# A graph and expert network on one Trainium2 core: ScalarE normalises every fourth tile of each LayerNorm

## The reference, cut to what matters

```python
def _layernorm(x, axis=-1, eps=1e-05):
    m = jnp.mean(x, axis=axis, keepdims=True)
    v = jnp.var(x, axis=axis, keepdims=True)
    return (x - m) / jnp.sqrt(v + eps)

x = x + L0_gnn(_layernorm(x));  x = x + L0_ffn(_layernorm(x))
x = x + L1_gnn(_layernorm(x));  x = x + L1_ffn(_layernorm(x))
...                             # the same for L2 and L3
```

## Time and profile before

| | us |
|---|---|
| median of three runs | 5675.14 |
| the profiled execution's own time | 5700.08 |
| its span | 5698.0 |
| PE busy | 4359.2 (77%) |
| DVE busy | 3235.9 (57%) |
| ACT busy | 2114.7 (37%) |
| POOL busy | 1202.7 (21%) |

### The profile page before, as it was taken

The page is one execution under the profiler, slowest core; times in us unless marked ns, Lnnn a source line. Parts: engine busy times, 40 slices in busy tenths (PEclk is TensorE's granted clock), DMA queues, the critical chain, the costliest instruction groups (busy, mean ns, idle before and its releaser), DMA issues. The chain is left out here.

```text
span 5698.0 us, 58897 instructions
## 1 busy us (share of the span) xinstructions
PE 4359.2 (77%) x18640; PEld 2870.1 (50%) x18640; DVE 3235.9 (57%) x6106; ACT 2114.7 (37%) x4158; POOL 1202.7 (21%) x1467
## 2 busy tenths in 40 slices
PE   1447355996784988879998898998787596889477
PEld 1335244775111767767775222223576465666366
DVE  7867244114897559731115898995787245453423
ACT  0003122113783045522223887888555011111222
POOL 1566666650220001000000111110010210000142
PEclk9868777997787989979998898899898798999788
DMA  8204243116443745320001443443453235462276
GB/s 351 103 1 162 93 134 88 39 38 208 158 155 113 241 167 196 117 45 0 0 0 58 157 156 124 165 159 94 164 191 128 88 109 177 148 199 90 107 221 203
DMA packets 460063, 733.30 MB, mean 129 GB/s; under 512 B 114081, under 2 KB 258974, under 8 KB 453004
## 3 DMA queue, kind: packets, MB, share of 16 engines
q1 hardware_dynamic: 410012, 690.18, 36.8%
q0 software_dynamic: 30096, 19.30, 1.2%
q10 hardware_dynamic: 19680, 20.48, 1.1%
HBM read 587.26 MB, written 147.21 MB: 129 GB/s over the span
## 5 line engine op out<-in xcount | busy, mean ns | idle before, releaser
L1459 PE MATMUL l2g_a_agg_acc<-all_x,l2g_a_h 128*65 128x512 f32 (+1 forms) x1400 | 644.3, 585 | 23.8 <-ACT l2g_a_agg_flat L1484 21.1
L429 POOL DMA_INDIRECT table<-first_count,first_cell x416 | 449.0, 1079 | 385.9 <-DVE first_cell L377 148.8
L1556 DVE SCALAR_TENSOR_TENSOR all_x<-all_x,l2g_a_agg_counts 128x512 f32<-128x512 f32 (+1 forms) x700 | 404.6, 625 | 121.6 <-ACT all_x L1507 121.0
L1496 ACT ACTIVATE l2g_a_agg_z<-l2g_a_agg_z 128x512 f32<-128x512 f32 (+1 forms) x700 | 344.3, 538 | 141.1 <-PE l2g_a_agg_z L1439 115.8
L1507 ACT ACTIVATE all_x<-l2g_a_agg_z 128x512 f32<-128x512 f32 (+1 forms) x700 | 353.7, 569 | 0.1
L2039 DVE SCALAR_TENSOR_TENSOR all_x<-l1f_moe_py,l1f_gate,all_x 128x256 f32 x200 | 96.7, 483 | 442.5 <-PE l1f_moe_py L1996 442.5
L892 PE MATMUL l3g_agg_acc<-l3g_agg_halves,l3g_agg_exact 128*128 128x512 f32 x1250 | 304.4, 398 | 51.6 <-DVE l3g_agg_exact L945 46.6
L1459 PEld LDWEIGHTS l2g_a_agg_acc<-all_x,l2g_a_h 128*65 128x65 f32 x1400 | 169.3, 144 | 285.9 <-issue 206.1
L1690 PE MATMUL l1g_gat_agg_acc<-l1g_gat_h,l1g_gat_agg_p 128*128 128x257 f32 x1250 | 284.8, 388 | 21.1 <-DVE l1g_gat_agg_p L1777 14.2
L1690 PE MATMUL l2g_b_agg_acc<-l2g_b_h,l2g_b_agg_p 128*128 128x257 f32 x1250 | 283.3, 387 | 19.6 <-DVE l2g_b_agg_p L1777 12.8
L2023 ACT ACTIVATE l1f_moe_hid<-l1f_moe_ph,l1f_vec 128x640 f32<-128x640 f32 x160 | 141.3, 883 | 420.9 <-PE l1f_moe_ph L2010 420.9
(11 more groups left out here) (790 smaller groups left out, 9264.8 us busy)
## 6 DMA issues: line engine op xcount, KB each, us to landing
l3g_agg_counts<-table SPq DMA_DIRECT2D x250, 320.0 KB, 3.4
l2g_a_agg_counts<-table SPq DMA_DIRECT2D x300, 256.0 KB, 4.4
table<-counting_eye_rows SPq DMA_DIRECT2D x25, 1600.0 KB, 37.3
l0g_agg_counts<-table SPq DMA_DIRECT2D x125, 320.0 KB
l1g_agg_counts<-table SPq DMA_DIRECT2D x125, 320.0 KB, 3.4
l2g_a_mask<-far SPq DMA_DIRECT2D x50, 800.0 KB, 4.4
l1g_gat_agg_counts<-table SPq DMA_DIRECT2D x150, 256.0 KB, 3.9
l2g_b_agg_counts<-table SPq DMA_DIRECT2D x150, 256.0 KB
```

The costliest lines, as they stand in the source:

```text
L429: pool.indirect_dma_start(self.table, bass.IndirectOffsetOnAxis(ap=self.cell[:, b, p:p + 1], axis=0), self.count(b, p), None, bounds_check ...
L1459: pe.matmul(to, rhs(t, r * per + h), p[:, u % n_p, 0:n], start=(t == 0), stop=(t == nt - 1), skip_group_check=True).then_inc(summed, 1)
L1496: act.activation(z[:, u % nz, 0:n], z[:, u % nz, 0:n], ACT.Relu, scale=1.0 - SLOPE).then_inc(bent, 1)
L1556: dve.scalar_tensor_tensor(out=w, in0=w, scalar=1.0, in1=counts[:, b % n_counts, 0:n], op0=ALU.min, op1=ALU.mult).then_inc(weighted, 1)
```

## The change

In each LayerNorm, ACT normalises the tiles with t % 4 == 3 (six of the 25), as Identity(scale * x + bias) with scale = rstd and bias = -mean * rstd, both columns of one number a row. DVE computes that bias for all tiles in one instruction of 128x25 (`shift`) and normalises the other 19 tiles. ACT does tiles 3 and 7 before its first copy, and tile 11, 15, 19 and 23 behind its copies 0, 2, 4 and 6; in `l3g_ln` it does all six in a row. `turn_tiles` waits for DVE's count and, at each fourth tile, for ACT's. A LayerNorm stage has 11 semaphores where it had 9.

```diff
+        shift = s.sb("shift", [P, T])
...
+                dve.scalar_tensor_tensor(out=shift[:], in0=mv[:, :, 0], scalar=-1.0, in1=rstd[:], op0=ALU.mult, op1=ALU.mult
+                                         ).then_inc(shifted, 1)
                 for t in range(T):
-                    dve.tensor_scalar(xn[:, t, :], x[:, t, :], mv[:, t, 0:1], rstd[:, t:t + 1],
-                                      ALU.subtract, ALU.mult).then_inc(done, 1)
+                    if t % 4 != 3:
+                        dve.tensor_scalar(xn[:, t, :], x[:, t, :], mv[:, t, 0:1], rstd[:, t:t + 1],
+                                          ALU.subtract, ALU.mult).then_inc(done, 1)
...
-                if fm is not None:
-                    copy_turned(act, pt, fm, turned, out)
+                act.wait_ge(shifted, 1)
+
+                def normal(t):
+                    act.activation(xn[:, t, :], x[:, t, :], ACT.Identity, bias=shift[:, t:t + 1], scale=rstd[:, t:t + 1]
+                                   ).then_inc(act_done, 1)
+
+                for t in range(3, 8 if fm is not None else T, 4):
+                    normal(t)
+                for i, t in enumerate(range(0, T, 2) if fm is not None else ()):
+                    n = min(2, T - t)
+                    act.wait_ge(turned, i + 1)
+                    act.activation(fm[:, :, t * P:(t + n) * P], pt[:, i % 4, :, 0:n * P], ACT.Identity).then_inc(out, 1)
+                    if i % 2 == 0 and 2 * i + 11 < T:
+                        normal(2 * i + 11)
...
-            pe.wait_ge(written, t + n)
+            pe.wait_ge(written[0], t + n - (t + n) // 4)
+            if (t + n) % 4 == 0:
+                pe.wait_ge(written[1], (t + n) // 4)
```

More of the change, by code:

```diff
@@ L626, in layernorm @@
         size = s.sb("size", [P, T])
+        shift = s.sb("shift", [P, T])
         pt = s.ps("pt", [P, 4, KD, 2 * P])
-        with stage(nc, tag, "stat", "agg", "eps", "root", "step", "done", "turned", "out", "blank_set") as (
-                block, stat, agg, eps, root, step, done, turned, out, blank_set):
+        with stage(nc, tag, "stat", "agg", "eps", "root", "step", "done", "shifted", "act_done", "turned", "out",
+                   "blank_set") as (block, stat, agg, eps, root, step, done, shifted, act_done, turned, out, blank_set):
             if ahead:
@@ L690, in _ @@
                 def _(pe):
-                    turn_tiles(pe, xn, pt, c.ident, turned, out, done)
+                    turn_tiles(pe, xn, pt, c.ident, turned, out, (done, act_done))
 def turn_tiles(pe, nm, pt, ident, turned, out, written=None):
```

## The result

The changed kernel takes 5684.38 us in the median of 19 runs (5671.84 to 5696.34), the kernel before 5673.95 (5665.49 to 5679.11, 19 runs): ratio 1.0017, 95% interval 1.001 to 1.0023. It is slower by 0.17%, in the direction of the forecast (+3.1 us, 0.05%), inside its range (5669 to 5687), but three times its size.

A forecast was written before the change was run, and what follows sets the result against it. In stages with transposes, PE bounds the slow phase and ACT's copies the quick one; DVE ends `l3g_ln`. Stage terms of +4.86 and -1.79 gave +3.1 us, on the 5675.14 median 5678.2 us; range 5669 to 5687.

The forecast's parts named there:

- What bounds the stages: Stages with transposes: PE bounds the slow phase at 0.853 us a pair, then ACT's copies, one every 0.477 us.
- The idle times of `l0f_ln` and `l1g_ln`: ACT's gaps from the first quick copy on, 0.59 and 0.28 us: all that a faster DVE could give back there.
- The price of an instruction: ACT's Identity of 128x256 with two columns: 584 ns each, one every 0.49 us, bounds 0.31 and 0.58.
- The new DVE operation: One 128x25 operation ahead of the tiles in each LayerNorm, delaying all the rest by 0.15 us.
- `l3g_ln`: LayerNorm without copies, ended by DVE alone: 0.15 - 1.94 = -1.79 us, the next stage starting earlier.
- The stages with transposes: Late start, late copy and uncovered normalisations less ACT's idle time: +0.63 to +1.03 us each, `l1f_ln` 0.
- `l2g_ln`: With six slow distances only tile 23 falls after the clock's rise: 0.15 + 0.49 - 0.01 = +0.63 us.
- `l0g_ln`: First LayerNorm stage, taken as `l1g_ln`: +0.96 us, counted in full in the sum.
- Its two late copies: ACT waits of 1.64 and 2.25 us in `l0g_ln`, cause unknown, left as is; bounds -3.9 and +2 us.
- The barrier: Two more semaphores a LayerNorm move one barrier ahead of `l1g_t2`, none added: 0, bounds -1.2 and +1.2 us.
- the slower rival: TensorE's clock falls behind a longer ACT tail: 3.1 us in each of five next stages, 5693.8 us; chance 0.07.
- The rule against the trace: Stages with transposes: by the skill's rule PE stays at 0.853 us a pair, sum about -0.7; forecast followed the trace.

The follow-up runs named there:

- e5: Against the kernel before: DVE normalises all 25 tiles, ACT also does its six Identity instructions with columns into an unread spare tile; 1.0018.
- e7: Against the kernel before: the change with ACT taking only tiles 3, 7, 11 and 15, but all six in `l3g_ln`; 0.9998.
- e2: Against the kernel before: ACT's share in `l0g_ln` alone, the seven later LayerNorms as before; 1.0001.
- e4: Kernel before with 11 semaphores a LayerNorm instead of 9, two of them unused, nothing else changed; 0.9999 against the kernel before.
- e8: Against the kernel before: ACT takes ten of 25 tiles in `l3g_ln` alone, the seven other LayerNorms as before; 0.9994.
- e1: The whole change measured again, against the kernel before; 1.0007.
- e6: Against the kernel before: DVE normalises all 25 tiles, ACT also does six Identity instructions without scale and bias into a spare tile; 1.0008.
- e3: Against the kernel before: ACT's share in the seven LayerNorms from `l0f_ln` on, `l0g_ln` as before; 1.0004, medians 5678.61 against 5674.93.
- e9: The whole change measured a third time, against the kernel before; 1.0010.
- e10: Against the kernel before: ACT takes four tiles in the stages with transposes, ten of 25 in `l3g_ln`; 0.9992, 5671.12 against 5673.17 us.

## Why the prediction was right, and where not

**What bounds the stages** was right. ACT's chain of copies ends them, DVE doesn't (e5), and ACT's instructions behind the clock's rise are what costs (e7). The idle times of `l0f_ln` and `l1g_ln`, 0.59 and 0.28, were 0.08 too high: in an unbroken chain the last copy takes 0.46 (e7), not 0.38.

**The price of an instruction** was right: 0.584 us forecast from the bias and scale groups, 0.587 to 0.600 measured; 0.49 start to start forecast, 0.49 to 0.50 measured. The new DVE operation delays the tiles by 0.10 us (944.97 to 945.07) where I took 0.15.

**`l3g_ln`** was right: -1.83 for -1.79.

**The stages with transposes** came out at +0.56 to +1.07, for +0.63 to +1.03. `l0f_ln` is +0.68 in the first pair of profiles (20.97 to 21.65), as forecast, and +1.07 in the means. The profile that I worked from was not typical, with DVE's tiles at 8.46 us where e2, e4 and e8 have 8.18 to 8.26, and in e1 (22.25) the clock rises about four pairs later than in the first profile of the change. `l2g_ln` was too low by 0.2, because its six slow distances belong to one execution too: in e2 and e4 the clock rises earlier, the all-DVE stage is 20.6 instead of 21.4, and two normalisations are uncovered. Together the seven stages from `l0f_ln` on give +2.6, for +2.1.

**`l0g_ln`** was right in its stage (+0.94 for +0.96). The step from there to the sum was not worked out: I had asked what ends the stage and not what ends the stages behind it. `l0g_agg` ends with POOL's scatters and has a spread of 5 us of its own, so the +0.96 is neither shown to arrive nor shown not to; I leave it out of the sum below. Its two late copies were an accident of that execution: no other profile has them, and their 4 us weren't seen at the end of `l0g_agg`.

**The barrier** was right: one moves, none is added, 0 (e4).

**The clock of the next stages** is what was missing in size, +2.8 us. I had it as the slower rival, with 3.1 us in each of five stages, at 0.07. It is real and smaller, it sits in three places, and it does not come about as I put it. I had PE idle about 1 us longer at the stage's end; ahead of `l2f_r` that idle time went from 1.26 to 1.47 us, ahead of `l3f_r2` it stayed at 1.03. The first 5 us of `l2f_r` (length, PE busy, granted clock, DMA share, GB/s), in the kernel before and in e1:

```profile
4417.00:4422.00 5.00, 4.71 (x32) 0.76 0.02 5
```

```profile
4420.00:4425.00 5.00, 5.00 (x25) 0.50 0.00 0
```

In the kernel before, the router still has the higher clock for its first 2.5 us and drops then; in e1 it has it for 0.9. It then stays at 0.50 to its end.

What goes with it in all twelve profiles is how long ago the clock had risen within `l2f_ln`: 4.3 us ahead of the router in the kernel before (20.0 us long), 4.65 in e6 (20.3), 5.1 in e4 and e7 (20.7), 5.5 after the change (21.1), 5.9 in e1, e3 and e9 (21.4). The length of `l2f_ln` alone does not order them, for e4 has the shortest (22.47). Two normalisations between the rise and the stage's end lengthen that time: by 0.8 us from e4 to e1, whose clocks rise within 0.2 us of the same place. Part of the +1.17 may be chance, for the clock rose 0.9 us earlier in three of the four shared profiles than in three of the four others; compared at a like rise it is +0.7 (e1 against e4) and +1.1 (the first profile after against the one before).

The second, `l3f_r2` (+0.44), is of the same kind: its clock falls 3.7 to 4.0 us into it instead of 4.2 to 4.4.

The third is not behind a longer stage but behind the shorter one. In `l3g_agg`, 170 us of dense products, all five profiles with six tiles of `l3g_ln` on ACT (e7's too) have a fall of the clock in the middle; no profile without the share has one, nor have those with ten tiles (e8, e10). With e5 and e6, in which ACT works beside DVE, that is five with it and seven without. The same stretch after the change, and in the kernel before:

```profile
4900.00:4911.00 11.00, 10.37 (x44) 1.00 0.90 293
4911.70:4915.10 3.40, 3.40 (x9) 0.51 0.28 81
4916.00:4927.00 11.00, 11.00 (x50) 1.00 0.85 266
```

```profile
4911.70:4915.10 3.40, 3.40 (x16) 1.00 0.91 296
```

Nine products instead of sixteen in 3.4 us. The stage is 1.2 us longer, and so two thirds of what `l3g_ln` had won are gone. e7, with the same six tiles in `l3g_ln`, shows the fall 75 us into the stage instead of 107 to 138, and its stage is 0.7 us longer.

What PE did ahead of the fall can be read. After the change, and the same place in the kernel before:

```profile
4910.72 7.52 PE L910 MATMUL l3g_agg_acc<-l3g_agg_halves,l3g_agg_exact 128*128 128x512 f32 x24 [0.63 <-DVE l3g_rows L946]
```

```profile
4902.76 9.57 PE L892 MATMUL l3g_agg_acc<-l3g_agg_halves,l3g_agg_exact 128*128 128x512 f32 x40 [0.63 <-DVE l3g_rows L928]
```

PE sat idle for 0.63 us, waiting for DVE, and the clock fell 0.9 us behind that wait; that is also why PE is busy for 10.37 of the 11.00 us above and not for all of them. In the four other profiles with a fall it begins 0.75 to 1.03 us behind such a wait. All twelve profiles have these waits at the same places of the stage (43, 74, 106 and 137 us into it, to within 1 us), and seven go through them at 1.00. So the wait belongs to it and isn't enough. The other thing that separates the two sets is where the clock rises at the stage's start: 7.0 to 8.1 us into it in the five, 8.4 to 9.3 in the seven. Why that should matter 70 to 130 us later is not shown.

**The sum.** The range's lower end, 5669, lies 2 us below what its own terms give (5678.2 - 7.2 = 5671.0), which decided nothing. +2.6 from the LayerNorms and +2.8 from the three stages is +5.4 us, 1.0010. That this lies so near the forecast's +3.1 is in part luck: the forecast counted 0.96 us that nothing shows to arrive and left out 2.8. The three measurements are 1.0017, 1.0007 and 1.0010; the first one's interval starts at 1.001 and overlaps with those of the two others. Whether its 4 us above the stages' sum are chance or something on that chip that no profile shows stays open. The profiles can't settle it: single long stages that the change leaves alone, such as `l1f_moe` (552 to 564 us), differ by more than that between executions.

**The rule against the trace.** The Trainium skill, "TensorE: Matmul & The Clock Gate", Part 4, has transposes without the full clock, and by that rule ACT's work would have been hidden. After the change too the clock rises within each of the seven stages of transposes, in `l0f_ln` to a mean of 0.83, and the transposes go from one every 0.213 us to one every 0.109; in e5 the work was not hidden. The trace decides.

## What to carry to other kernels

Before work is moved to an engine that is idle 63% of the span, look at that engine inside the stage: here it had 0.0 to 0.5 us to spare behind the point where the transposes get fast, and six instructions took 2.9. An engine's tiles can be given away at a gain only in the stage that this engine itself ends, and then in the ratio of the start-to-start times (15 to 10 here, for 0.32 and 0.49 us), columns included. A stage's own sum is not the kernel's: ask what the stages behind it wait for, a running scatter or the clock.

## What the runs showed of the hardware that I had not expected

- A 170 us stretch of products can lose the higher clock for 3.4 us (9 products for 16) with nothing changed in its own instructions: in all five profiles of one split of the stage ahead of it, in none of the seven others. Each time it begins 0.75 to 1.03 us behind a wait of PE of 0.63 us, a wait that the seven others have as well. What decides between them is not shown.
- How long a stage keeps the higher clock can be set in the stage before: the router behind `l2f_ln` keeps it for 2.5 us when it had risen 4.3 us ahead of it, for 0.9 when 5.9.
- Where the clock rises in a run of transposes moves by up to three pairs, 2.6 us, between executions of the same stage. That alone spreads an unchanged LayerNorm stage by 0.8 us (20.6 to 21.4 in `l2g_ln`), as much as the change costs it.
- The printed clock is 1.00 wherever the trace has no record yet, here up to 217 to 219 us. The distance between instructions of one shape (0.213 against 0.109 us) shows the clock that was there.
- An ACTIVATE of 128x512 out of PSUM follows the one before after 0.477 us, although each lasts 0.60.
